# The second half's grouped convolutions as 32 by 32 tiles of the array, in a fused conditioned-convolution and feed-forward kernel

## What is computed

```python
def _L0_cond_ref(x, c, weight, c_weight, bias):
    out = lax.conv_general_dilated(x, weight, window_strides=(1,), padding=[(4, 4)],
                                   dimension_numbers=('NCH', 'OIH', 'NCH'), feature_group_count=4)  # 9 taps
    ctx = jnp.einsum('nd,od->no', c, c_weight)
    return out + ctx[:, :, None] + bias[None, :, None]

def _L0_ffn_ref(h, gate_w, up_w, down_w, fc1_w, fc2_w, expert_w, ln_gamma, ln_beta):
    routing_weights, _ = jax.lax.top_k(h @ gate_w, 2)
    shared_out = (jax.nn.relu(h @ up_w) ** 2) @ down_w               # 512 -> 1024 -> 512
    routed_out = (((h @ fc1_w) @ expert_w) * routing_weights.sum(-1, keepdims=True)) @ fc2_w
    return layernorm(shared_out + routed_out)

x = x + _L0_ffn_ref(_L0_cond_ref(...))
x = x + _L1_ffn_ref(_L1_cond_ref(x, ...))   # softmax over 8 kernels of a per-sample 32 by 32 mix; low-rank experts
```

## Time and profile before

| what | value |
|---|---|
| median of 3 runs | 221.2 us (217.3, 221.2 and 221.25) |
| the profiled execution | 217.5 us, of which the span of the profile is 215.7 us |
| PE busy | 211.2 us, 98% of the span |
| DVE, ACT, POOL busy | 124.8, 80.1 and 61.8 us |
| granted PE clock | 1.00 in every slice |
| DMA | 14.94 MB, mean 69 GB/s |

### The profile page before, as it was taken

How to read it: one execution, slowest core, us unless ns; L and a number is a source line. 1 busy time by engine, 2 the same in 40 slices (tenths; PEclk the granted TensorE clock), 3 DMA queues, 4 the chain that set the end, 5 groups by cost and what they waited for, 6 DMA issues and landing times.

```text
span 215.7 us, 3106 instructions
## 1 busy us (share of the span) xinstructions
PE 211.2 (98%) x1155; PEld 183.4 (85%) x1155; DVE 124.8 (58%) x265; ACT 80.1 (37%) x156; POOL 61.8 (29%) x77
## 2 busy tenths in 40 slices
PE   7999899999999999999999999999999999999994
PEld 7997778888887789987888888888998998999984
DVE  4979356869525455597852034456996537435443
ACT  5998555369384612222222034431013112121110
POOL 3018421340475620021960012442264202202000
PEclk9999999999999999999999999999999999999999
DMA  6999655310000000174645000000000110110104
GB/s 177 346 406 406 219 116 109 61 27 0 0 3 0 0 0 3 25 123 68 91 41 146 0 0 0 3 0 2 0 3 0 49 49 3 50 49 0 52 0 146
DMA packets 31455, 14.94 MB, mean 69 GB/s; under 512 B 25336, under 2 KB 26168, under 8 KB 31440
## 3 DMA queue, kind: packets, MB, share of 16 engines
q1 hardware_dynamic: 30624, 14.05, 23.4%
q10 hardware_dynamic: 816, 0.69, 1.5%
HBM read 12.62 MB, written 2.11 MB: 68 GB/s over the span
## 4 chain that ended last, share of the span: by engine, by line
PE 95%; DVE 4%; issue 0%; DVEq 0%
PE PS L1214 26%; PE PS L1216 25%; PE PS L1215 25%; PE PS L1233 9%; PE PS L1341 3%; PE PS L1403 2%; DVE up_lo L864 1%; DVE H_lo L885 1%; PE PS L1258 1%; PE PS L1257 1%; PE PS L1412 1%; PE PS L1370 0%; PE PS L1267 0%; DVE ex_lo L997 0%; DVE up_hi L993 0%; PE PS L1456 0%
## 5 line engine op out<-in xcount | busy, mean ns | idle before, releaser
L910 DVE TENSOR_TENSOR PS<-PS,relu 128x512 f32<-128x512 f32 x16 | 11.2, 699 | 30.9 <-ACT relu L675 30.9
L1214 PE MATMUL PS<-H_hi,up_hi 128*128 128x512 f32 x64 | 25.6, 399 | 0.5 <-DVE H_lo L885 0.5
L1216 PE MATMUL PS<-H_hi,up_lo 128*128 128x512 f32 x64 | 25.0, 390 | 0.0
L1215 PE MATMUL PS<-H_lo,up_hi 128*128 128x512 f32 x64 | 25.0, 390 | 0.0
L1233 PE MATMUL PS<-wconv,XS 128*128 128x128 f32 x192 | 22.4, 276 | 0.0
L1233 PEld LDWEIGHTS PS<-wconv,XS 128*128 128x128 f32 x192 | 21.9, 192 | 0.3
L1216 PE MATMUL PS<-qkT_hi,H_lo 128*128 128x320 f32 x64 | 19.8, 309 | 0.0
L1215 PE MATMUL PS<-qkT_lo,H_hi 128*128 128x320 f32 x64 | 19.8, 309 | 0.0
L1214 PE MATMUL PS<-qkT_hi,H_hi 128*128 128x320 f32 x64 | 19.7, 308 | 0.0
L675 ACT ACTIVATE relu<-PS 128x512 f32<-128x512 f32 x16 | 9.5, 594 | 25.5 <-PE PS L1216 23.0
L595 POOL TENSOR_TENSOR X<-X,rowb 128x512 f32<-128x512 f32 x8 | 10.3, 1297 | 28.1 <-PE PS L1341 28.1
(11 more groups left out here) (187 smaller groups left out, 459.6 us busy)
## 6 DMA issues: line engine op xcount, KB each, us to landing
up_raw<-in_L_ffn_up_w_dram SPq DMA_DIRECT2D x2, 1024.0 KB, 8.9
dn_raw<-in_L_ffn_down_w_dram SPq DMA_DIRECT2D x2, 1024.0 KB, 13.0
out_dram<-X SPq DMA_DIRECT2D x7, 256.0 KB, 2.0
X<-in_x_dram SPq DMA_DIRECT2D x1, 1024.0 KB, 13.9
XS<-in_L_ffn_W_dram SPq DMA_DIRECT2D x16, 64.0 KB, 2.3
X<-in_x_dram SPq DMA_DIRECT2D x2, 256.0 KB, 2.9
X<-in_x_dram SPq DMA_DIRECT2D x1, 512.0 KB, 5.4
fc<-in_L_ffn_fc_w_dram SPq DMA_DIRECT2D x1, 512.0 KB, 5.7
```

What stands on the lines that cost most here:

```text
L910: nc.vector.tensor_tensor(U[i % 2], U[i % 2], relu[:], ALU.mult).then_inc(s_sq, 1)
L1214: nc.tensor.matmul(o, lh, rh, start=start, stop=False)
L1215: nc.tensor.matmul(o, lh, rl, start=False, stop=False)
L1216: return nc.tensor.matmul(o, ll, rh, start=False, stop=stop)
```

## The change

1. The second half's convolutions are no longer 48 matmuls on the whole array with a weight matrix that is mostly zeros. `group_convs()` issues 48 float32 matmuls of 32 rows by 32 columns, each with 512 moving columns: 3 windows by 4 tiles `t` by 4 groups `g`. The rows are the 8 channels of a group in 4 phases (partitions 32g on), the columns go to partitions 32t of bank `conv_bank(4 + g)`. Their result has the output channel and phase in the partition, and the position in the free dimension.
2. So the context is one number per partition, sample and group (`bctx`). ACT adds it with a bias in 4 copies of 128 by 128 (group 0), DVE with a broadcast in 3 of 128 by 512 (groups 1 to 3), into `wide`; `turn_groups()` then turns it back with 16 transposes on PE, and `split_H` reads the banks. `add_ctx` is gone.
3. The input of the tiles has the channels of a group together. ACT and DVE write it by phases into `wide` in 2 copies each of 128 by 512 (in place of `shift_copies(3)`), and SP sends it through DRAM: 4 DMAs out, 16 back into `XS`. The weights `wgrp` come from `wconv` by 16 small DMAs within SBUF, and one copy on POOL brings them in order (`s_wgrp`). The context rows go out in 4 DMAs after a small copy on POOL.
4. PE's order: `group_convs` stands ahead of `down(6)`, `turn_groups` between `down(6)` and `down(7)`. The conditioning moves earlier, so that the banks are free: its steps stand after `routed`, after `down(2)`, after `up(5)`, after `up(6)` and after `down(4)`. ACT's gelus go to chunks 4 and 5, `exp_att` behind chunk 5; `split_wk` from chunk 5 to 4.
5. POOL clears `BD` after the convolutions, since its place is `wide`.

The tile matmuls and the transposes, and where PE's order calls them:

```diff
+            def group_convs():
+                pe.wait_ge(s_wgrp, 1)
+                pe.wait_ge(ld_xs, 16 * G * PH)
+                pe.wait_ge(s_R, IC)
+                pe.wait_ge(s_lat, LC)
+                pe.wait_ge(s_agg, 2)
+                pe.wait_ge(s_aggb, 1)
+                for a in range(NWIN):
+                    for t in range(TPH):
+                        for g in range(G):
+                            gs = slice(C * g, C * (g + 1))
+                            last = nc.tensor.matmul(conv_bank(TPH + g)[C * t:C * (t + 1), :],
+                                                    wgrp_op[gs, a],
+                                                    XS[gs, :, a:a + P].rearrange("k (s t) m -> k t s m", t=TPH)[:, t],
+                                                    start=(a == 0), stop=(a == NWIN - 1))
+                last.then_inc(s_grp, 1)
+            def turn_groups():
+                pe.wait_ge(s_ga, SPT)
+                pe.wait_ge(s_gv, G - 1)
+                for s in range(SPT):
+                    view = conv_bank(TPH + s).rearrange("m (t p g o) -> m g t o p", p=PH, g=G, o=CG)
+                    for g in range(G):
+                        last = nc.tensor.transpose(view[:, g], wide[:, g, s * P:(s + 1) * P], ident[:])
                     last.then_inc(s_conv, 1)
...
                 if h:
-                    conv(TPH)
-                    for t in range(1, TPH):
-                        conv(TPH + t)
+                    group_convs()
+                    down(IC - 2)
+                    turn_groups()
                     down(IC - 1)
...
-                for c in range(IC if h else IC - 1):
+                for c in range(IC if h else IC - 2):
                     down(h * IC + c)
                     if c == 1:
                         routed(h)
-                    if h == 0:
-                        conditioning(c)
+                    if h == 0 and c == 1:
+                        cond_layer0()
+                    if h == 0 and c == 2:
+                        cond_layer1()
+                    if h == 0 and c == 4:
+                        mixing()
                     if c + 3 < IC:
                         up(h * IC + c + 3)
+                    if h == 0 and c == 2:
+                        cond_logits()
+                    if h == 0 and c == 3:
+                        turn_att()
```

On POOL, behind its loop over the chunks of the first half, and on SP, behind the loads of the weights that `turn_group` needs:

```diff
+            pool.wait_ge(ld_wgrp, 16 * G * PH)
+            nc.gpsimd.tensor_copy(wgrp_op.rearrange("k a (o p) -> k a p o", p=PH),
+                                  wgrp.rearrange("k a (p o) -> k a p o", p=PH)).then_inc(s_wgrp, 1)
             for T in range(TPH):
                 norm_scale(T)
+            pool.wait_ge(s_conv, TILES)
+            nc.gpsimd.memset(BD, 0.0).then_inc(s_zero, 1)
...
+            for g in range(G):
+                for j in range(PH):
+                    sp.dma_start(XS[C * g + CG * j:C * g + CG * (j + 1), :, 1:1 + P],
+                                 xph_rows[j, CG * g:CG * (g + 1)].rearrange("c s t m -> c (s t) m")).then_inc(ld_xs, 16)
```

More of the change, by code:

```diff
@@ L266, in bass_adaln_ffn @@
         s_rows = sem("s_rows")
+        s_rowsp = sem("s_rowsp")
         s_foldz = sem("s_foldz")
@@ L315, in bass_adaln_ffn @@
         s_conv = sem("s_conv")
-        s_tf = sem("s_tf")
+        ld_wgrp = sem("ld_wgrp")
+        s_wgrp = sem("s_wgrp")
+        s_xpw = sem("s_xpw")
+        ld_xs = sem("ld_xs")
+        s_grp = sem("s_grp")
+        s_ga = sem("s_ga")
+        s_gv = sem("s_gv")
         s_Hh = sem("s_Hh")
@@ L757, in _ @@
                 if h:
-                    for t in range(TPH):
-                        split_H(TPH + t)
+                    act.wait_ge(s_grp, 1)
+                    act.wait_ge(s_B0, 16)
+                    for s in range(SPT):
+                        nc.scalar.activation(wide[:, 0, s * P:(s + 1) * P], conv_bank(TPH)[:, s * P:(s + 1) * P],
+                                             ACT.Identity, bias=bctx[:, s, 0:1]).then_inc(s_ga, 1)
+                    for s in range(SPT):
+                        split_H(TPH + s)
                 up_relu(i0)
@@ L1056, in _ @@
                 if h:
-                    split_attT()
-                    copy_aggb()
-                    turn_agg()
+                    dve.wait_ge(s_grp, 1)
+                    dve.wait_ge(s_B0, 16)
+                    for g in range(1, G):
+                        nc.vector.tensor_tensor(wide[:, g].rearrange("q (s m) -> q s m", s=SPT),
+                                                conv_bank(TPH + g).rearrange("q (s m) -> q s m", s=SPT),
+                                                bctx[:, :, g].unsqueeze(2).broadcast_to([P, SPT, P]), ALU.add)\
+                            .then_inc(s_gv, 1)
                     for T in range(TPH, TILES):
-                        add_ctx(T)
                         split_H(T)
@@ L1449, in mixing @@
                 pe.wait_ge(s_aTl, 1)
[L1450 to L1452 removed]
+                nc.tensor.matmul(M[0][N:2 * N, 0:C], attT2[:], bk[:], start=True, stop=True).then_inc(s_aggbp, 1)
                 pe.wait_ge(s_wk, 1)
```

152 lines of the change are left out of this document (80 added, 72 removed).

## The result

The changed kernel takes **219.16 us** (median of 12 runs, 218.01 to 219.52), where the kernel before took 217.75 beside it (12 runs: seven at 216.99 to 217.75, five at 221.15 to 222.25). The ratio is 1.0072, with a 95% interval of 1.0056 to 1.0089: slower by 0.7%, within the 2%. The forecast was 237 us. The mechanism is that of its first rival, all sixteen tiles beside each other (218.4); that the two numbers lie within 0.8 us is luck, since three of its terms were off and largely cancelled (see the point by point part).

A forecast was written before the change was run, and what follows sets the result against it. PE's own list was taken to bound the kernel. The sum was 217.5 - 10.7 + 21.4 + 1.8 + 1.6 + 3.7 = 235.3 us, plus 1.9 for half the run gap: 237 us, range 217 to 242.

The forecast's parts named there:

- first rival: At group_convs, all sixteen tiles run beside each other, 4.5 us; whole kernel 218.4 us, chance 0.28.
- What goes: Second half's old convolutions save 10.7 us of PE; dropping add_ctx and twelve shifted input copies is worth 0.
- X: Time of the 96 tile matmul records in group_convs; taken as in pairs, 21.4 us, each operation costing one record.
- my own sign: At the tile group, the forecast is wrong if its 96 records take under 8 us.
- My fourth line: Tile matmuls with all sixteen tiles beside each other: 2.7 us of streaming, but issue binds, taken as 4.5 us.
- T: Sixteen 128 by 128 transposes on PE cost 1.8 us, or 3.5 if the strided output doubles the step.
- Logits: PE waits 1.6 us at the logits for the second gelu, queued behind split_wk, weight group 0 and a split_dn.
- Tile weights: Ahead of group_convs, PE waits 3.7 us (3.3 to 4.1) for POOL's copy of the weights behind group_split(3).
- Costed at nothing: Weight, context and XS transfers through DRAM, about 0.5 us an issue; reads land by 67, 10 us of cover.
- Start: At the first relu, three more DMA issues delay the context rows by 0 to 0.5 us, with slack.
- The clock: PE's 3.7 us wait could bring back the lower clock, adding about 1.5 us; counted in the upper bound only.
- Half the gap: On the total, 1.9 us added, since two of three runs shown were 3.7 us over the profiled one.

The follow-up runs named there:

- wgrp_early: Changed kernel with GpSimd's copy of the tile weights moved into its loop, ahead of split_dn(5); 217.63 us, ratio 1.001.
- fold_first: Changed kernel with GpSimd waiting for the fold product before it computes fc2_lo; 219.13 us, ratio 1.0081.
- best2: Changed kernel with the edits of wgrp_early and gelu_early, mixing behind up(7), and the sixteen reads of XS issued as four; 214.04 us, ratio 0.9867.
- one_tile: Changed kernel with all 48 tile matmuls on the array's first tile, each a result of its own, other results left out; 297.73 us, one run.
- gelu_early: Changed kernel with ScalarE's second gelu moved ahead of split_wk; 219.47 us, ratio 1.0105.
- warm10: Changed kernel with ten warming matmuls of TensorE at the start instead of seven; 219.51 us, ratio 1.0082.
- same_tile: Changed kernel with the loops of group_convs turned round, so each tile's three matmuls follow each other directly; 246.96 us, one run.
- cond_only: Kernel before with only the conditioning moved earlier, convolutions as they were; 220.27 us, ratio 1.0108.
- one_row: Changed kernel with all tile matmuls reading channel group 0, so only the first row group's four tiles are used; 260.44 us, one run.
- one_col: Changed kernel with all tile matmuls writing the first column group, each a result of its own, so four tiles are used; 226.77 us, one run.
- xs_early: wgrp_early with SyncE's writes of xph_rows ahead of the last twelve Wk loads and XS read in four issues; 217.63 us, ratio 0.9986.
- best3: best2 with GpSimd waiting for VectorE's fold product before it computes fc2_lo; 214.86 us, ratio 0.9873.

## Why the prediction was wrong, point by point

- **What bounds the kernel** (PE's own list; every wait put into it costs its length): right. It is why 5.6 us less of PE work (10.7 - 3.4 - 1.7) brought no gain against 4.6 us of new waits and a later start. In wgrp_early, fold_first and best2 the chain up to the tile group runs through SP's queue and no longer through PE.
- **What goes, 10.7 us; copies and add_ctx worth 0**: right.
- **X, the step that failed**: "in pairs", 21.4 us, measured 3.4. The ground was that the second record of an operation has to wait for its tile and that, since records start strictly in turn, everything behind waits as well. The first half is right (one_tile: one record at a time). The second is not: 32 weight loads went in within 0.24 us, and the first records of all sixteen tiles started within 0.12 us, ahead of second records that stand earlier in the program. By my own sign (under 8 us) the forecast was wrong. Starts in turn on the whole array say nothing of tiles, since there all records want the same tile. The Trainium skill, "TensorE: Matmul & The Clock Gate", Part 3, had both a rule of order and a measured factor of 10.6; I weighted the rule over the number. The trace disagrees with the rule and agrees with the number, with two records of a matmul on a tile as well: 42.9 us in turn (by one_tile's 0.43 a record, 41) became 3.4, a factor of 12.
- **My fourth line, 4.5 us by issue**: closest, still high. Records in a burst start 0.008 to 0.02 us apart, not 0.04 to 0.07. So issue did not bind: the time is six steps of streaming.
- **T, 1.8**: 1.75 (chain) to 1.91 us; the strided output costs nothing. All that was hidden under `down(6)` and `down(7)` stayed hidden.
- **Logits, 1.6**: 1.57. As a price on the total it was right in the sum but not alone: gelu_early took it away and gained nothing. No wait at mixing: right.
- **Tile weights, 3.7**: 2.97. The copy took 0.35 where I took 0.9 (0.5 to 1.3); the chain ahead of it came as forecast. Wgrp_early's 2.3 us less of waiting brought 1.5 us in the median (219.16 to 217.63).
- **Costed at nothing, the way through DRAM**: mis-sized by 14 us. Forecast: reads landed by 67 with 10 us of cover. Measured: 0.74 and 0.69 us an issue instead of 0.5, writes landed only at 61.9 because SP left the Wq and Wk blocks at 55.7 instead of 52, and the last read flew 8.5 us. It landed at 81 to 82, 1 to 2 us ahead of the end of GpSimd's copy (83.05): the next wait stood directly behind the one I named. The sign "it waits for the blocks of XS" came true in the runs with an early start (4.4 us in fold_first, 4.8 in warm10).
- **Start, 0 to 0.5**: 2.4 us in the profile. Same_tile, alike up to there but with the early form, started up(0) at 22.59: so 2.15 us are the late form, and 0.3 are left, which is less than the early starts differ among themselves (21.8 to 22.6). The late form also occurs where only the conditioning was moved (cond_only); whether the change makes it more frequent isn't known.
- **The clock, 1.5 us**: not in the changed kernel's profile (1.00 behind both waits). Where it came, in fold_first, it cost 2.1 us in the tile group alone (5.5 in place of 3.4).
- **Half the gap, 1.9 us**: wrong in kind. The changed kernel's 12 runs have no such gap; that XS and the clock swallow it is argued above, not shown.
- **The range, 217 to 242**: it holds the result only because it was stretched to the all-sixteen rival. Its ends don't quite follow from the terms: the likeliest's own lower end comes to 233.7 and the upper to 243.0, not 233 and 242.

With X at 3.4, T at 1.75 and waits of 1.6 and 3.0 the forecast's own sum gives 217.5 - 10.7 + 9.75 = 216.6 us, and the start's 2.4 us make it 219.0, of 219.16 measured. The rival's 218.4 came near by luck: 1.1 us too much for the tiles and 0.7 for their weights stood against 2.4 too little at the start.

## What to carry to other kernels

When a measured factor and a rule contradict each other, and the trace has no such operation, the factor deserves more weight than a mechanism built from rows of another kind. Cycle small tiles so that neighbouring operations use different ones: here two records in a row on one tile cost next to nothing, six and eight in a row took the time of two steps and of four. And when a chain is moved ahead of work on the bounding engine, write down the next two chains behind it with their landing times, small DMAs through DRAM above all: here removing a wait of 2.97 us laid bare one of 0.69, and one of 1.57 reappeared as 1.47. And before two variants are compared, look whether their profiles start alike: here the start alone moved the time by 2 us and more, as much as most of the edits.

## What the runs showed of the hardware

- 96 fp32 records of 512 columns over sixteen 32 by 32 tiles, six on each and never more than two in a row on one, ran in 3.4 us, 12 times as fast as one tile would. The same work ordered tile by tile (six in a row) ran about three records at a time, and in one_row, with eight in a row, two at a time.
- Work on one tile does not keep TensorE's clock: in one_tile it was at 0.73 over 84 to 86 us, and at 0.50 from then on, though PE was busy throughout. Two and three tiles at a time (one_row, same_tile) also stayed at 0.50; with four (one_col) it was back at 1.00 from 86 us on, and with all sixteen it never fell in the changed kernel's profile.
- A wait of PE can bring the clock down, and its length alone does not decide: 1.82 us in cond_only was followed by 0.50, 4.43 in fold_first as well, 2.97 in the changed kernel and 2.75 in xs_early were not.
- The small copies of weights between partitions took 0.74 us of SP's queue each and the 64 KB reads of XS 0.69, against 0.48 to 0.51 for the 32 KB blocks of Wq and Wk. The last of sixteen reads of XS needed 8.5 us to land; four reads of 256 KB took 9 us of queue and 10 of flight.
- A 32x32 operation of VectorE took 2.45 us while GpSimd ran a two-input operation of 2.34 us, against 0.18 in fold_first, best2 and best3, where GpSimd's began later. A CAST of 64x32 took 3.77 us in cond_only, beside GpSimd's operation and the clears behind it, against 0.17 in the other profiles.
